# One shared transposition for h1 of two blocks and one for h2, in the third to last pairs of a four-layer adapter kernel

## What is computed

```
L0: W = weights[condition];                       y = einsum('bct,bcd->bdt', x, W)      # mixes the 64 tokens
L1: y = x @ W + (x @ lora_A[i]) @ lora_B[i]                                             # rank 16, one of 16 adapters per sequence
L2: y = x @ W.T + 0.5 * (x @ lora_A[j]) @ lora_B_w.T                                    # rank 32, one of 5 per sequence
L3: logits = x @ Wr.T + bias of 5 at the language's expert; top 2 of 8; gates = softmax of the two
    y = x @ W.T + 2 * sum over e, r of (x @ A[e])[r] * gates[e] * B[e][:, r]            # 8 experts of rank 16
x = x + L0(x);  x = x + L1(x);  x = x + L2(x);  x = x + L3(x)
```

## Times and profile before

| | us |
|---|---|
| median of 3 runs | 520.22 |
| lowest, highest | 519.98, 522.53 |
| the profiled execution, its own time | 520.41 |
| its span, first to last instruction | 518.6 |
| TensorE busy | 513.6 |
| VectorE busy | 326.3 |
| ScalarE busy | 208.2 |
| GpSimd busy | 171.8 |
| tokens' part (from the first token product) | 240 to 518.6 |

### The profile page before, as it was taken

How to read it: one execution, slowest core, us unless ns; L and a number is a source line. 1 busy time by engine, 2 the same in 40 slices (tenths; PEclk the granted TensorE clock), 3 DMA queues, 4 the chain that set the end, 5 groups by cost and what they waited for, 6 DMA issues and landing times.

```text
span 518.6 us, 8860 instructions
## 1 busy us (share of the span) xinstructions
PE 513.6 (99%) x2715; PEld 449.2 (87%) x2715; DVE 326.3 (63%) x655; ACT 208.2 (40%) x366; POOL 171.8 (33%) x250
## 2 busy tenths in 40 slices
PE   8999999999999999999999999999999999999997
PEld 7999999988988888888887888888888888888886
DVE  3798886799533333389877864655645656447464
ACT  4744653345122323268344343333443334334322
POOL 2550000002102021219548544444255334552400
PEclk9999999999999999999999999999999999999999
DMA  7921210214430202040604304223142042240402
GB/s 251 375 76 40 61 40 1 82 40 124 158 114 0 82 0 82 0 166 5 229 15 136 105 17 139 85 64 124 50 144 94 20 135 82 97 142 0 152 1 81
DMA packets 29632, 46.81 MB, mean 90 GB/s; under 512 B 12052, under 2 KB 17940, under 8 KB 29476
## 3 DMA queue, kind: packets, MB, share of 16 engines
q1 hardware_dynamic: 29268, 45.72, 26.6%
q0 software_dynamic: 192, 0.59, 0.3%
q10 hardware_dynamic: 144, 0.13, 0.1%
HBM read 33.39 MB, written 13.04 MB: 90 GB/s over the span
## 4 chain that ended last, share of the span: by engine, by line
PE 95%; POOL 2%; DMA 1%; SPq 1%; issue 0%; ACT 0%; POOLq 0%
PE bank L2043 26%; PE bank L1977 15%; PE bank L1909 11%; PE bank L2032 8%; PE bank L1951 6%; PE bank L1963 5%; PE bank L2135 4%; PE bank L1880 4%; PE bank L2103 4%; PE bank L2111 4%; PE bank L1864 3%; PE bank L2106 1%; PE bank L2105 1%; DMA w2raw<-in_w_dram 1%; PE bank L2053 1%; POOL em_lo L704 1%
## 5 line engine op out<-in xcount | busy, mean ns | idle before, releaser
L2043 PE MATMUL bank<-t_hi,em_hi 128*128 128x512 f32 x168 | 57.0, 400 | 0.0
L700 POOL CAST em_hi<-tba 128x256 fp32r x32 | 13.4, 447 | 82.5 <-PE bank L2032 78.9
L714 POOL TENSOR_TENSOR tmp<-raw 128x512 f32<-128x512 f32 x4 | 7.2, 1791 | 97.3 <-DVE raw L1460 97.3
L2043 PEld LDWEIGHTS bank<-t_hi,em_hi 128*128 128x128 f32 x168 | 31.1, 189 | 6.5
L1977 PE MATMUL bank<-te,em_hi 128*128 128x512 f32 x144 | 34.9, 395 | 0.0
L1274 DVE TENSOR_TENSOR w1t_lo<-raw,w1t_hi 128x1024 fp32r<-128x1024 f32 x18 | 22.6, 1255 | 17.1 <-ACT w1t_hi L939 17.1
L1977 PEld LDWEIGHTS bank<-te,em_hi 128*128 128x128 f32 x144 | 27.0, 188 | 6.5
L1274 DVE TENSOR_TENSOR em_hi<-tmp,em_hi 128x512 fp32r<-128x512 f32 x22 | 15.3, 693 | 21.1 <-ACT em_hi L1046 12.0
L704 POOL TENSOR_TENSOR em_lo<-tba,em_hi 128x256 fp32r<-128x256 f32 x32 | 26.9, 862 | 2.4 <-POOL em_hi L700 1.2
L1274 DVE TENSOR_TENSOR em_lo<-bank,em_hi 128x232 fp32r<-128x232 f32 (+2 forms) x36 | 16.7, 484 | 16.6 <-ACT em_hi L1062 13.0
L1909 PE MATMUL bank<-em_hi,w2s_hi 128*128 128x384 f32 x80 | 27.0, 337 | 0.0
(11 more groups left out here) (320 smaller groups left out, 1625.1 us busy)
## 6 DMA issues: line engine op xcount, KB each, us to landing
raw<-in_x_dram SPq DMA_DIRECT2D x16, 512.0 KB, 3.9
b1s<-b1scr SPq DMA_DIRECT2D x32, 217.5 KB, 2.8
raw<-in_b1w_dram SPq DMA_DIRECT2D x10, 512.0 KB, 3.4
out_dram<-ef SPq DMA_DIRECT2D x16, 256.0 KB, 2.1
out_dram<-ost SPq DMA_DIRECT2D x15, 256.0 KB, 2.2
graw<-in_w3a3wr_dram SPq DMA_DIRECT2D x4, 768.0 KB, 11.0
b1scr<-b1stage SPq DMA_DIRECT2D x12, 256.0 KB
w2raw<-in_w_dram SPq DMA_DIRECT2D x6, 384.0 KB, 7.0
```

Of the source, the lines that this page charges most:

```text
L2043: ins = nc.tensor.matmul(to[:, :], left[a][:, k0 + k, :], m_right(right, z, k), start=(name in OPENS and n == 0), stop=(n == 3 * KH - 1), ...
```

## The change

In pairs 2 to 7 (the loop's body, and the last pair now too) h1 of both blocks goes into one tile `h11c` of 128 columns and through one transposition; h2 of both goes into `h2c` (hi and lo of each block) and through another. Both stand where the shared one stood, in p7 and p3. h1 of b0, which was transposed in p1 and used in p5, now goes with b1's. The repeats are made by ScalarE: four copies for h1, six for h2, three of them ahead of left_hi and three behind. The zeros of h1 are written each time: VectorE multiplies both sequences' rows by a column of `head` (1 in the rows of the sequence, 0 in the others), 128 rows at a time in place of 64. `head` is set by four memsets in the first pair. `gated_across` of b0 moves from p4 into the narrow behind it (in the last pair it stays in p4), and in the last pair that of b1 moves from behind tile 0 to behind tile 1. The cores of the diff, with the bookkeeping of the semaphores left out:

```diff
+            def h1_both_t(p):
+                act.wait_ge(s_th, skewed_turns(p) + 1)
+                for s in range(2):
+                    at_ = s * H1_COLS
+                    nc.scalar.activation(h1T[s][0:H1_COLS, :], bank[RT + 1][at_:at_ + H1_COLS, Z1], ACT.Copy).then_inc(s_hts, 1)
+                    nc.scalar.activation(h1T[s][H1_COLS:2 * SEG1, :], bank[RT + 1][at_:at_ + PER * R1, Z1], ACT.Copy).then_inc(s_hts, 1)
...
@@ VectorE @@
-                    steps.then(V.tensor_copy(H1_NEXT[ts, 0, :, h], nar[ts, at_:at_ + R1]))
+                    steps.then(V.tensor_scalar(H1_BOTH[:, s, 0, :, h], nar[:, at_:at_ + R1], head[:, h:h + 1], None, ALU.mult))
                 steps.hold()
...
-                    lo(H1_NEXT[ts, 1, :, h], nar[ts, at_:at_ + R1], H1_NEXT[ts, 0, :, h], s_h1c)
+                    V.scalar_tensor_tensor(H1_BOTH[:, s, 1, :, h], nar[:, at_:at_ + R1], head[:, h:h + 1], f32(H1_BOTH[:, s, 0, :, h]),
+                                           ALU.mult, ALU.subtract).then_inc(s_h1c, 1)
...
@@ VectorE, the order of a pair @@
+                h1_of(p, 1, steps)
+                h2_of(p, 0, steps)
+                h2_of(p, 1, steps)
+                sum_p7(p)
+                xm_lo(0, bank[BA], 4 * p + 1)
+                route(b0, 0, steps, 6 * p + SMALL["h2", 0])
+                if not last:
+                    left_lo(p + 1)
+                gates(b0, 0, steps)
+                route(b1, 1, steps, 6 * p + SMALL["h2", 1])
+                ght_lo(b0, 0)
+                xm_lo(1, bank[BD_], 4 * p + 2)
+                gates(b1, 1, steps, b0 + 1)
+                if not last:
+                    xn_lo(b0 + 2, YB + 1)
...
@@ TensorE @@
-                part("p1", 5, 11)
-                h1_across(b0, 0)
-                part("p1", 11, 12)
+                part("p1", 5, 12)
                 pe.wait_ge(s_opl, ops + 2)
-                part("p5", 0, 9)
-                h1_into_from(copies + 1, 0, p)
-                part("p5", 9, 12)
+                part("p5", 0, 12)
...
+                    part("p4", 4, 12)
+                    pe.wait_ge(s_opl, ops + 7)
+                    narrow(b0 + 2, first_block, YB + 1, range(0, 3))
+                    gated_across(b0, 0)
+                    narrow(b0 + 2, first_block, YB + 1, range(3, K))
```

More of the change, by code:

```diff
@@ L1192, in pair_hi @@
                 xm_hi(0, bank[BA])
-                if not last:
-                    left_hi(p + 1)
+                left_hi(p + 1)
                 h2_t(b1, 1)
@@ L1198, in pair_hi @@
                 exp_of(b1)
[L1199 to L1200 removed]
+                xn_hi(b0 + 2, YB + 1)
                 ght_hi(b1, 1)
@@ L1722, in first_pair_lo @@
                 V.memset(f32(h1c[:, :]), 0.0).then_inc(s_z, 1)
+                for h in range(PER):
+                    for ts in range(PER):
+                        V.memset(head[ts * T:(ts + 1) * T, h:h + 1], 1.0 if ts == h else 0.0).then_inc(s_z, 1)
                 xn_lo(0, YB)
@@ L1792, in pair_lo @@
                 xm_lo(0, bank[BA], 4 * p + 1)
-                if not last:
-                    left_lo(p + 1)
-                    xm_lo(1, bank[BD_], 4 * p + 2)
+                left_lo(p + 1)
+                xm_lo(1, bank[BD_], 4 * p + 2)
                 route(b1, 1, steps)
-                if last:
-                    xm_lo(1, bank[BD_], 4 * p + 2)
                 gates(b1, 1, steps)
-                if not last:
-                    xn_lo(b0 + 2, YB + 1)
+                xn_lo(b0 + 2, YB + 1)
                 ght_lo(b1, 1)
@@ L2021, in _, with narrow @@
                 rows_pair(j)
-            def narrow(b, left, to):
-                pe.wait_ge(s_sel, 4 * b + 4)
-                if isinstance(b, int) and b == 0:
-                    pe.wait_ge(s_s0l, 1)
-                above(pe, s_xnl, b)
-                for k in range(K):
+            def narrow(b, left, to, ks=range(K)):
+                if ks.start == 0:
+                    pe.wait_ge(s_sel, 4 * b + 4)
+                    if isinstance(b, int) and b == 0:
+                        pe.wait_ge(s_s0l, 1)
+                    above(pe, s_xnl, b)
+                for k in ks:
                     for a, z in TERMS:
@@ L2287, in pair_products @@
-                if not last:
-                    pe.wait_ge(s_opl, ops + 7)
-                    narrow(b0 + 2, first_block, YB + 1)
-                if not last:
-                    gated_across(b1, 1)
-                tile(p, 0, False, last)
-                if last:
-                    gated_across(b1, 1)
-                for n in range(1, 3 if last else 4):
-                    tile(p, n, False, last)
-                if last:
-                    last_tile(p)
-            def skewed_pair_products(p):
+                part("p7", 0, 8)
@@ new lines, in pair_products @@
+                gated_across(b0, 0)
+                part("p7", 8, 12)
+                pe.wait_ge(s_opl, ops + 6)
+                part("p3", 0, 2)
+                h1_across(b1, 1)
+                part("p3", 2, 6)
+                h1_into(b1, 1, p)
+                part("p3", 6, 12)
+                pe.wait_ge(s_add, sums + 3)
+                there("t4")
+                part("p4", 0, 1)
+                h2_across(b1, 1)
+                part("p4", 1, 7)
+                h2_into(b1, 1)
+                part("p4", 7, 12)
@@ L2301, in skewed_pair_products @@
+                pe.wait_ge(s_opl, ops + 7)
+                narrow(b0 + 2, first_block, YB + 1)
+                gated_across(b1, 1)
+                for n in range(4):
+                    tile(p, n, False, False)
+            def skewed_pair_products(p, last):
                 b0, b1 = 2 * p, 2 * p + 1
@@ L2358 @@
+            with pe.Fori(SKEWED.start, NP - 1) as p:
+                skewed_pair_products(p, False)
+            skewed_pair_products(NP - 1, True)
 _OUTS = [((32, 64, 1024), "float32")]
```

286 lines of the change are left out of this document (118 added, 168 removed).

## The result

| | before | after |
|---|---|---|
| median of the runs, us | 520.19 (519.77 to 522.53, 14 runs) | 521.23 (520.68 to 521.63, 14 runs) |
| the profiled execution, us | 520.41 | 521.33 |
| its span, us | 518.6 | 519.5 |

The ratio of after to before is 1.0015, with a 95% interval of 1.0008 to 1.0022. The change makes the kernel slower by 0.15%, about 1.0 us. That is inside the range of the prediction and within its bound of 0.5%, but I had forecast 0.3 us faster, and the measurement excludes that.

The account below looks back on a forecast made before the run. TensorE, busy 99% of the span, was taken to bound the kernel. -0.77 + 0.54 - 0.06 = -0.29 us took the median from 520.22 to 519.9 us, range 519.1 to 521.4.

Parts of the forecast that it names:

- Seven transpositions go: TensorE's stream: one transposition fewer in each of five loop pairs, two in the last, at 0.11 us: -0.77 us.
- The first wait: Shared h1 transposition in p7, waiting for VectorE's masked h1: 0.2 us left, no cost, at most 0.05.
- What follows the first wait: From shared h1 transposition to first block's h1_into: spacing of 1.03 us taken as unchanged, no wait named.
- The second wait: Shared h2 transposition, waiting for VectorE's two h2 blocks: gap of 0.09 us in each of six pairs, +0.54.
- Behind it: After the shared h2 transposition: ScalarE's copies, h2_into and the first block's gates all in time, no cost.
- The third place: Gated transposition inside the narrow, chain to tile 1: 0.2 us left, no cost, thinnest place after the second wait.
- The last pair: Tile 2, late before, no longer has ScalarE's copy behind the second block's gated one: -0.06 us.
- the memsets: Four at the start, under 0.56 us, within VectorE's idle time of 1.72 us: nothing.
- a dearer transposition in the narrow: Gated transposition between narrow products: taken at 0.11 us, up to +0.1 in each of five pairs, +0.5, as upper bound.
- Rival 1: Shared h2 transposition doesn't wait; the whole -0.77 - 0.06 arrives, 519.4 us; chance 0.27.
- rival 2: VectorE's two h2 blocks in a row take longer, tile 1's margin is spent too: +2.0, 522.2 us; chance 0.19.
- Rival 3: Second block's h2 copies on ScalarE, behind left_hi, come late because x lands late: +3.5, 523.4 us; chance 0.04.

Follow-up runs that it names:

- e4: Kernel before, with the first block's gated transposition issued three times more in p4 of each loop pair; median 522.10 us against 520.33, ratio 1.0041.
- e1: Changed kernel, with GpSimd's casts for the next pair's second block held until the second block's gates are done; median 520.47 us against 520.33 of before, ratio 0.9997.
- e3: Changed kernel, with the waits for b1s of both blocks moved ahead of p7, out of h1_into; median 521.01 us against 520.33 of before, ratio 1.0014.

## Why the prediction was right or wrong

- **"Seven transpositions go", -0.77.** Right. Distances in e4 give 0.113 each.
- **The first wait (shared h1), no cost.** Right, with more to spare than I took: the masked pairs of 128 rows took 0.38 each, not 0.48. Two such instructions overlap: the second starts 0.15 behind the first, which takes 0.23. By the Trainium skill (VectorE: DVE Perf Modes, section on two Vector instructions with no wait between them) an instruction is not held for the one ahead when both start in the same quadrant of rows, and the trace agrees with that.
- **What follows the first wait.** Here the prediction took over a distance of 1.03 from transposition to small product from the earlier trace rows and took it that its load had waited 0.17 "without delaying the product". That was true, but by 0.01: the load may come 0.93 after the transposition, and it came 0.92 after in the kernel before. In after the wait for the copy stands on an instruction of its own and the load comes 0.99 after. I had counted instructions and not looked at which of them carries the wait. This step was missing from the sum, and it is worth +0.33.
- **The second wait (shared h2), +0.54.** The mechanism was right, VectorE's two blocks took the 1.75 us that I gave them, and the load came 0.05 after. It measured 0.06 instead of 0.09, +0.38: the two sums of eight terms were off by 0.03. One of them was added up wrongly: 399.12 + 0.10 + 5 x 0.23 is 400.37 and not 400.39, so that the recorded terms give 0.11.
- **"Behind it", no cost.** Right for ScalarE's copies, h2_into and the first block's gates: the gated transposition starts at once when TensorE gets to it. (ScalarE's copy of p7 would end at 400.12 + 0.60 = 400.72 by the prediction's own rows, not at 400.6, and the second three copies nearer 403.6 than 403.4; neither decided anything.)
- **"The third place ... No cost."** This is the step that failed, and it is worth 1.04 of the 1.21 us by which the two sums differ; h1_into's 0.33 less the 0.16 of the second wait are the rest. I had 410.57 - 410.4 = 0.17 us left. It took the gates as 1.50 us, from a block that had no GpSimd beside it, and a load 0.05 behind its releaser. Measured were 1.76 and 0.12: 0.33 more than I had counted, less the 0.17, is the 0.16 that tile 1 was late. (Term by term: the steps add up to 3.44 and were rounded to 3.5. Measured were 3.80, from the gated transposition at 407.49 to 411.29, against 3.64 that TensorE takes to the due start at 411.13.) I called it the thinnest place and then gave it no term. In the first pair of the loop it is 0.40; e1 takes 0.23 of that away, and the 0.17 left come from VectorE's idle time ahead of gm, whose own cause stays open.
- **The last pair, -0.06; the memsets, nothing.** Right.
- **The rivals.** Rival 1 (no second wait) fell: the wait is there in each pair. Of rival 2, the first half (VectorE's h2 blocks longer, by waits on registers or by a shared bank) fell, since they took 1.74 us. Its second half, tile 1's margin spent, is what happened, by a mechanism that I had not seen and at 0.16 instead of 0.1. It should have been a rival of its own, with VectorE and GpSimd side by side looked at in the trace of before: in pair 4 the casts start 0.6 us behind the gates' end, and in pair 1 the lengthened gates were there to be read. Rival 3 didn't occur. The prediction's last sentence, that a waiting load of tile 1 would show a lost margin, is what the trace showed.
- **The range.** Its upper end, 521.4, leaves out a term that it names: 520.22 - 0.77 - 0.06 + 6 x 0.25 + 0.5 is 521.39, and with 0.3 for a median 521.7. The median of 521.23 lies in it either way, and by luck: the room was allowed for a second wait of 0.25, which was 0.06, and for a dearer transposition in the narrow, which cost 0.11 as among wide products. Neither bound was meant for the wait of tile 1, which filled it.

## What to carry to other kernels

When a change moves a step of one engine past the start of another engine's block, look at what will now run side by side, and take durations from rows that had the same company. A margin of under 0.3 us against a sum of ten terms is not "no cost": give it a term, or move the step until it has more; here 6 narrow products sooner gave back 0.15 us in each pair. Removing work from a saturated TensorE pays only if every product that waits keeps its load's slack, so write down for each how late its weight load may come (here its due start less 0.11), and compare that with what ends ahead of it.

## What the runs showed of the hardware

- **GpSimd beside VectorE.** Some steps of VectorE are held until an instruction of GpSimd that is already running ends: beside casts of 128x256 the 128x8 gate step took 0.30 us instead of 0.17 and a pair of masks 0.58 instead of 0.48, and each lengthened step ended 0.02 to 0.03 behind a cast's end. It goes the other way too: a cast of 128x12 that began during a 1.22 us subtraction of VectorE took 0.56 instead of 0.19.
- **A wait on its own.** A weight load starts 0.05 to 0.06 us behind the end of what it waits for where the product carries that wait (before, e3), and 0.12 behind where the wait stands on an instruction ahead of it and the product carries another.
- **Lateness of a load.** A product of 512 columns is on time when its weight load starts 0.11 us ahead (409.16 for 409.27, the first of tile 0 in after). Tile 1's load came 0.16 later than that and its product was 0.16 late.
- **A 128-column transposition** costs 0.113 us in a stream of wide products, and 0.11 among narrow ones: 407.38, 407.49 and 407.52 are the starts of a narrow product, the transposition and the next narrow product in after, and 407.71 the one behind, 0.33 for three.
